# A Mamba-and-attention block: products in halves of rows, and where transposes and turned scores stand

## What is computed

```python
xn = layernorm(x)
# branch 1: D_INNER 512
u = xn @ W_in + b_in
u = causal_conv(u, conv_w, 4 taps) + conv_b
h = tanh(A) h + u_t * Bp;  y_t = Cp h + Dp u_t     # 16 states, scanned over 512 steps
branch1 = silu(y) @ W_out + b_out
# branch 2: 16 heads of 16 columns
q, k, v = xn @ W_qkv + b_qkv
attn = softmax(q k^T / 4) @ v
gate = softmax(xn @ W_gate + b_gate);  combine = the two largest of 8, others 0
branch2 = attn + sum_e combine[e] * (xn @ W_experts[e] + b_experts[e])
out = x + branch1 + branch2
```

## Time and profile before

| | |
|---|---|
| median of 3 runs | 786.23 us (785.99 to 787.51) |
| span of the profiled execution | 784.0 us |
| the profiled execution's own time | not listed beside its span |
| PE busy | 756.4 us, 96% |
| VectorE busy | 582.2 us, 74% |
| ScalarE busy | 534.5 us, 68% |
| GpSimd busy | 389.7 us, 50% |

### The profile page before, as it was taken

One profiled execution on the slowest core, in us unless ns is written; L12 is line 12 of the kernel. 1 busy time (PEld: TensorE's weight loads), 2 busy tenths in 40 slices (PEclk: granted clock), 3 DMA queues, 4 the chain that ended last, 5 costly groups with the idle time before them and its releaser, 6 DMA issues.

```text
span 784.0 us, 13236 instructions
## 1 busy us (share of the span) xinstructions
PE 756.4 (96%) x4408; PEld 455.7 (58%) x4408; DVE 582.2 (74%) x846; ACT 534.5 (68%) x926; POOL 389.7 (50%) x522
## 2 busy tenths in 40 slices
PE   9889999999999999999999999989999999999996
PEld 7566656566555665556555565556655565555553
DVE  6679785977679765897759877698767987568920
ACT  5546775676666766777667776667666776767775
POOL 8347482456344834455346373445444473435654
PEclk9979999999999999999999999999999999999999
DMA  8302111122110221102111121103111111112000
GB/s 272 68 8 66 46 24 30 30 69 69 35 29 22 69 69 41 42 15 82 42 42 42 42 86 32 39 23 96 42 42 43 42 49 41 46 39 69 22 2 27
DMA packets 32465, 39.09 MB, mean 50 GB/s; under 512 B 8513, under 2 KB 18535, under 8 KB 32398
## 3 DMA queue, kind: packets, MB, share of 16 engines
q1 hardware_dynamic: 31418, 37.29, 18.1%
q10 hardware_dynamic: 980, 0.96, 0.6%
HBM read 8.74 MB, written 4.19 MB: 17 GB/s over the span
## 4 chain that ended last, share of the span: by engine, by line
PE 80%; DVE 13%; issue 3%; POOL 2%; ACT 2%; DMA 0%; ACTq 0%; DVEq 0%; POOLq 0%
PE PS L464 38%; PE PS L624 13%; PE SB L591 12%; PE TB L608 7%; PE PS L521 4%; DVE mx L1049 4%; DVE xn L1026 2%; DVE ys L900 2%; PE PS L480 2%; DVE qkl L926 1%; POOL acc L1118 1%; PE PS L631 1%; DVE xl L932 1%; PE PS L476 1%; PE PS L555 1%
## 5 line engine op out<-in xcount | busy, mean ns | idle before, releaser
L1049 DVE TENSOR_REDUCE mx<-SB 128x2 f32<-128x1024 f32 x256 | 312.6, 1221 | 145.2 <-PE SB L591 144.3
L1118 POOL TENSOR_TENSOR acc<-acc,mt 128x256 f32<-128x256 f32 x320 | 252.7, 798 | 244.4 <-ACT mt L674 181.7
L827 ACT ACTIVATE Pt<-TB 128x1024 f32<-128x1024 f32 x251 | 257.5, 1026 | 58.1 <-PE TB L608 54.5
L674 ACT ACTIVATE mt<-PS,cpad 128x256 f32<-128x256 f32 x256 | 107.4, 470 | 58.5 <-PE PS L464 56.5
L591 PE MATMUL SB<-kst,qst 48*128 48x512 f32 x512 | 128.2, 497 | 12.1 <-DVE mx L1049 11.7
L624 PE MATMUL PS<-Pt,V 128*17 128x512 f32 x1024 | 122.3, 595 | 0.0
L591 PEld LDWEIGHTS SB<-kst,qst 48*128 48x128 f32 x512 | 47.8, 183 | 122.4 <-DVE mx L1049 70.3
L464 PE MATMUL PS<-weh,xTh 128*128 128x512 f32 x256 | 109.8, 429 | 1.9 <-DVE xTl L913 1.2
L608 PE MATMUL TB<-qst,kst 50*128 50x512 f32 x502 | 101.3, 399 | 1.3 <-ACT Pt L827 1.3
L464 PE MATMUL PS<-wel,xTh 128*128 128x512 f32 x256 | 100.9, 394 | 0.0
L464 PE MATMUL PS<-weh,xTl 128*128 128x512 f32 x256 | 100.7, 393 | 0.0
(11 more groups left out here) (162 smaller groups left out, 1138.9 us busy)
## 6 DMA issues: line engine op xcount, KB each, us to landing
qst<-qkh SPq DMA_DIRECT2D x124, 64.0 KB, 2.3
kst<-qkh SPq DMA_DIRECT2D x124, 64.0 KB, 2.3
out<-acc SPq DMA_DIRECT2D x8, 512.0 KB, 2.8
qst<-qkl SPq DMA_DIRECT2D x62, 64.0 KB, 2.2
kst<-qkl SPq DMA_DIRECT2D x62, 64.0 KB, 2.3
acc<-in_x SPq DMA_DIRECT2D x7, 512.0 KB, 3.9
Bt<-in_wexp SPq DMA_DIRECT2D x2, 512.0 KB, 8.0
raw<-in_wexp SPq DMA_DIRECT2D x2, 512.0 KB, 8.5
```

Source lines behind the costliest of these rows:

```text
L674: return e.activation(mt[:, item % NM, :], P, ACT.Copy, scale=scale)
L827: e.activation(Pt[:, T % NP, :, :], turned_bank(T)[:, :, :], ACT.Exp, scale=0.25).then_inc(s_ex, 1)
L1049: e.tensor_reduce(mx[:, g % 2, 0:2, 4 * jj + a], SB[:, :, :], AX.X, ALU.max).then_inc(s_mx, 1)
L1118: e.tensor_tensor(v, v, mt[:, item % NM, :], ALU.add).then_inc(s_mt, 1)
```

## The change

Products of V, Q, Z, Y, M and O are issued as halves of 64 rows. `side_by_side(u)` issues the lower halves (rows 0:64) of unit u, and between them the upper halves (rows 64:128) of the unit ahead, whose lower ones are done (s_low); low and high count the columns that each half of the array has been given, and an upper half is issued when its count is behind. Upper ones that are left stand between the two products of the next pair of scores. The planner knows for each unit where it starts and where it is done (ENDS), and a unit keeps its bank for both. X and P move to t divisible by 8 behind the values, T and C to t % 8 == 4 behind values; LAG is 12, so values also stand at t divisible by 4. In a step with two split units `turned` stands between them, otherwise behind `score` as before. X is a plain product of 16 columns in place of a transpose of 72. Z's results have tiles of their own (before they lay over xh and xl). The planner's costs are changed, and the scratch size for DMA descriptors is 1024 rather than 8192.

```diff
-LAG = 11
+LAG = 12
...
+SETTLE = 1500
-COST = {"T": 0.45, "V": 0.75, "Q": 1.42, "Z": 2.05, "Y": 1.42, "C": 0.45, "M": 1.42, "O": 1.5, "B": 0.25, "D": 1.42,
-        "X": 0.15, "P": 0.45}
-
-VECTOR = {"T": {1: 0.7}, "V": {1: 0.2}, "Q": {1: 0.8}, "Z": {1: 1.4}, "P": {1: 0.7}, "X": {1: 0.3},
-          "Y": {2: 1.1, 3: 1.1, 4: 1.1, 5: 1.1, 6: 0.85}}
+Unit = namedtuple("Unit", "kind b i t done read bank use frees item before split")
+
+COST = {"T": 0.45, "V": 0.72, "Q": 1.38, "Z": 1.95, "Y": 1.38, "C": 0.45, "M": 1.38, "O": 1.5, "B": 0.25, "D": 1.42,
+        "X": 0.2, "P": 0.45}
+
+VECTOR = {"T": {1: 0.7}, "V": {2: 0.2}, "Q": {2: 0.8}, "Z": {2: 1.4}, "P": {1: 0.7}, "X": {1: 0.3},
+          "Y": {3: 1.1, 4: 1.1, 5: 1.1, 6: 1.1, 7: 0.85}}
...
+def normal_at(t):
+
+    g, rest = divmod(t - LAG - 12, 8)
+    if t == STEPS + LAG + 2:
+        return NG - 1
+    return g if rest == 0 and 0 <= g < NG - 1 else None
+
+
+def in_halves(kind, b, i, t):
+
+    return kind in "VQZYMO" and t > 1 and (kind, b, i) != LAST
...
-        return 0.43 * pairs + 0.8 * len(values_at(t))
+        return 0.23 * pairs + 1.1 * len(values_at(t))
+
+    def whole_at(t):
+
+        return t % 8 == 4 or t < LAG
...
-        spent = min(spent, 1.0) + share + 0.7 * max(vector[t] - share, 0.0) - fixed(t) - sum(COST[u[0]] for u in row)
+        spent = min(spent, 1.0) + share + 0.35 * max(vector[t] - share, 0.0) - fixed(t) - sum(COST[u[0]] for u in row)
...
+        g = normal_at(t)
+        if g is not None:
             row.append(("P", g // 4, g))
+        halves = 0
+        while t != STEPS + LAG - 2:
+            k = next((k for k, u in enumerate(todo) if soonest(*u) <= t
+                      and (whole_at(t) if u[0] in "TC" else not values_at(t))), None)
+            if k is None:
+                break
+            if todo[k][0] not in "TCB" and (spent < COST[todo[k][0]] / 2 - 1.2 * bare or len(row) > 2):
...
+            if in_halves(*u, t):
+                if open_ is not None:
+                    done[open_] = t
+                open_ = u
+                halves += 1
+            else:
+                done[u] = t
...
+        if open_ is not None and not halves and not values_at(t):
+            done[open_] = t
+            alone.add(t)
+            open_ = None
...
+            bank = min((j for j in range(3) if j != open_), key=lambda j: used[j])
+            used[bank] = place[key]
...
-    return AT[t - 1][-1:] if t - 1 in AT else []
+    return ENDS[t - 1][-1:] if t - 1 in ENDS else []
...
+        zh = sb("zh", [128, 2, 512], F32R)
+        zl = sb("zl", [128, 2, 512], F32R)
...
-        mx = sb("mx", [128, 2, 9, 8])
+        mx = sb("mx", [128, 2, 2, 8])
...
+            def products(u):
+
+                P, b, i = FB[u.bank], u.b, u.i
+                xh_, xl_ = xTh[b % 2], xTl[b % 2]
+                if u.kind == "V":
+                    ts = slice(128 * i, 128 * i + 128)
+                    for f in range(2):
+                        for v, w in ((xh_, wvh), (xl_, wvh), (xh_, wvl)):
+                            yield P[:, 0:264], v[:, f, ts], w[:, f, :], True
...
+            def rest_of_ahead(until=None):
+
+                nonlocal ahead, done, high
+                while ahead and (until is None or high <= until):
+                    o, a, w, _ = ahead_rows[done]
+                    if done == 0:
+                        e.wait_ge(s_low, lower_done)
+                    ins = e.matmul(o, a[64:128], w[64:128], start=False, stop=(done == len(ahead_rows) - 1),
+                                   skip_group_check=True)
+                    high += max(w.shape[1], 256)
+                    done += 1
+                    if done == len(ahead_rows):
+                        ins.then_inc(s_full[ahead.bank], 1)
+                        ahead = None
+
+            def side_by_side(u):
+
+                nonlocal ahead, ahead_rows, half, done, low, high, settled, slots, lower_done
+                rest_of_ahead()
+                ahead, done, high, lower_done = half, 0, max(high, settled), slots
+                half = u
+                if ahead is None:
+                    high = low
+                else:
+                    ahead_rows = [p for p in products(ahead) if p[3]]
+                if u is None:
+                    return rest_of_ahead()
+                start = True
+                for o, a, w, _ in products(u):
+                    rest_of_ahead(low - 1)
+                    ins = e.matmul(o, a[0:64], w[0:64], start=start, stop=False, skip_group_check=True)
+                    start, settled = False, low + SETTLE
+                    low += max(w.shape[1], 256)
+                ins.then_inc(s_low, 1)
+                slots += 1
+                rest_of_ahead(low - 1)
+
+            def bank_there(u):
+                if u.before is not None:
+                    if ahead is not None and ahead.bank == u.bank:
+                        rest_of_ahead()
+                    e.wait_ge(*bank_read(u.before))
...
+                    ins = e.matmul(P[0:16, 0:128], mx[:, i % 2, :, :].rearrange("p h c -> p (h c)"), ident[:, :],
+                                   start=True, stop=True)
...
             def score(t):
...
                 for h in range(2):
                     rows = slice(64 * h, 64 * h + 48)
+                    if h:
+                        rest_of_ahead()
...
                 ins.then_inc(s_S, 1)
+                pair_behind()
...
+            def pair_behind():
+                nonlocal low, high
+                low, high = max(low + 512, high), max(low, high) + 512
 
             def values(m):
+                nonlocal low, high
                 g, a = m // 4, m % 4
+                rest_of_ahead()
+                low = high = max(low, high) + 2200
...
+                between = [u for u in AT[t] if u.split][1:]
+                if LAG <= t < STEPS + LAG and not between:
                     turned(t - LAG)
                 for m in values_at(t):
                     values(m)
+                if t in ALONE:
+                    side_by_side(None)
                 for u in AT[t]:
-                    unit(u)
+                    if between and u is between[0] and LAG <= t < STEPS + LAG:
+                        turned(t - LAG)
+                    if u.split:
+                        bank_there(u)
+                        operands_there(u)
+                        side_by_side(u)
+                    else:
+                        unit(u)
...
-                e.wait_ge(*full("Z", b, 0))
+                    if b and i == 0:
+                        e.wait_ge(*full("Y", b - 1, 3))
+                    e.copy(zh[:, i, :], P[:, :]).then_inc(s_zh, 1)
...
-                    e.wait_ge(*full("Y", b - 1, 3))
+                    e.wait_ge(*full("Z", b - 1, 1))
...
+                    e.wait_ge(s_zh, 2 * b + i + 1)
+                    ins = e.tensor_tensor(zl[:, i, :], P[:, :], F(zh[:, i, :]), ALU.subtract)
```

More of the change, by code:

```diff
@@ L44 @@
          1: [("Q", 0), ("Q", 1)]}
+LAST = ("M", NB - 1, 15)
 def values_at(t):
@@ L152, in plan @@
+    finish = {u: (t, t + (k == len(row) - 1)) for t, row in ends.items() for k, u in enumerate(row)}
+    place = {u: n for n, u in enumerate(u for row in ends.values() for u in row)}
+    units, item, uses, frees, held = {}, 0, [0] * 3, [0] * 3, [None] * 3
+    used, open_ = [-9] * 3, None
     for t, row in steps.items():
         units[t] = []
-        for k, (kind, b, i) in enumerate(row):
-            bank = min((j for j in range(3) if free[j] <= t), key=lambda j: used[j])
-            n += 1
-            used[bank] = n
+        if t in alone:
+            open_ = None
+        for key in row:
+            kind, b, i = key
+            split = in_halves(*key, t)
+            bank = min((j for j in range(3) if j != open_), key=lambda j: used[j])
+            used[bank] = place[key]
@@ L158, in plan @@
             uses[bank] += 1
             frees[bank] += kind not in "MO"
[L160 to L165 removed]
+            u = Unit(kind, b, i, t, *finish[key], bank, uses[bank], frees[bank], item, held[bank], split)
@@ L166, in plan @@
             item += 2 * (kind in "MO")
             held[bank] = u
+            if split:
+                open_ = bank
             units[t].append(u)
-    return units, xh, ln
-AT, XH, LN = plan()
+    return units, {t: [next(u for u in sum(units.values(), []) if (u.kind, u.b, u.i) == k) for k in row]
+                   for t, row in ends.items()}, alone, xh, ln
+AT, ENDS, ALONE, XH, LN = plan()
 UNIT = {(u.kind, u.b, u.i): u for units in AT.values() for u in units}
@@ new lines, in in_one @@
+            def in_one(u):
+                rows = list(products(u))
+                for k, (o, v, w, _) in enumerate(rows):
+                    ins = e.matmul(o, v, w, start=(k == 0), stop=(k == len(rows) - 1))
+                return ins
+            def rest_of_ahead(until=None):
[11 more added lines that the diff above has]
+                        ahead = None
@@ L637, in _ @@
```

(3 more changed lines are left out.)

210 lines of the change are left out of this document (98 added, 112 removed).

## The result

The changed kernel takes 810.65 us (median of 4 runs, 807.96 to 812.04); the kernel before, measured beside it, 786.87 us (785.99 to 788.19). The ratio is 1.0299, with a 95% interval from 1.0276 to 1.0323: slower by 24 us, where 746 was forecast and 714 to 778 was the range.

A forecast was written before the change was run, and what follows sets the result against it. PE was taken as the bound, by its own work. Halves save 77 us, less 3 and 12, so 62; waits return 22: 784.0 - 62 + 22 = 744 as span, 746 as median; range 714 to 778.

The forecast's parts named there:

- a one-unit step: PE's step of scores, turned scores and one unit was to go from 2.25 to 1.85 us.
- Rivals 3 and 4: PE pays each half product's fixed part (38 us back, 784, chance 0.04); or exposes 0.05 per slot in loads (840, 0.09).
- The term for the transposes: X, P, T and C behind values on PE: added shape changes and exposed loads cost 12 us, ends 0 and 19.
- the gain of the halves: On PE, 192 steps each lose 0.40 us of drains and exposed loads: 77 us saved.
- term (b): Split units hold banks over two unit times, so readers get one instead of two: 12 us, bounds 0 and 45.
- rival 5: On PE, upper halves are left over and run alone; costed like the badly hidden loads and counted in their 0.09.
- (a) Maximum: Next scores wait for VectorE's maximum, delayed by convolution taps in shortened steps: 7 us of waits.
- (c) SyncE's queue: Stack DMAs and the block's store come late in SP's queue: 10 us, bounds 0 and 30.
- the first steps: Steps before about 20 wait for weight loads and DVE and give no gain: 3 us off the saving.
- overlap: Waits on maximum, banks and SP's queue let other engines catch up: of 29 us, 22 counted.
- rivals, 2: Queue of banks and stacks takes most, at two thirds of its bounds, 50 us: 774, chance 0.16.
- The one slower case: On PE, the two halves hide each other's loads badly, 0.05 us per slot, 94 us: 840, chance 0.09.

The follow-up runs named there:

- e10: Changed kernel with VectorE reading banks before the convolution taps, turned scores always straight behind the scores, and halves only from step 17 on: 789.63 us.
- e12: e10 with P, T and C in the places they had in the kernel before: 821.32 us.
- e1: Changed kernel with no unit split (whole products); LAG 12, places and new planner costs stay: 810.91 us.
- e2: e1 with units taking only two banks in turn instead of three: 843.71 us.
- e17: e1 with VectorE reading the bank before the convolution tap: 808.45 us.
- e4: Changed kernel with VectorE reading the bank of the unit that ended last before the step's convolution taps: 791.33 us.
- e7: Changed kernel with the three shifted convolution taps over only 8 columns: 787.51 us.
- e8: Kernel before with the three shifted convolution taps over only 8 columns: 778.05 us.
- e13: Kernel before with LAG 12 instead of 11, and the plan that it leads to: 807.21 us.
- e5: e1 with the planner's old costs, VectorE load table, fixed part and weight: 800.30 us.
- e11: e10 with the planner's old weight of VectorE's load, 0.7 for 0.35: 812.67 us.
- e9: e5 with P, T and C where they stood before, X staying behind values: 805.69 us.
- e14: Changed kernel with LAG 11; values, P and X moved to t % 8 == 7, T and C to t % 8 == 3: 820.21 us.

## Why the prediction was wrong

**What was right.** The halves' work on PE: pairs 0.23 apart, no drains, a one-unit step 1.86 for 1.85. X and P behind values at 2.63 for 2.61. Rivals 3 and 4 don't occur: the 1878 further products cost PE neither their fixed part nor exposed loads where both halves run. The rule of the Trainium skill, TensorEngine Tiling (Array Packing), Instruction Overhead, that each matmul carries about 60 cycles, isn't borne out for pairs by these starts either. The term for the transposes is 47 x 0.20 + 32 x 0.10 = 12.6, written as 12; nothing hangs on it.

**Two steps failed.** They are the gain of the halves, put at 77 us and measured at 33, and term (b), the banks, put at 12 us and measured at 33.

**The gain of 77 was too large.** It took a split unit to run in pairs always. Counted as for e10 to e12, between 100 and 770 us of the changed kernel, one half of the array runs alone for about 54 us and neither for 95. In e1 these are 4 and 115, drains and waits together. So halves take some 21 us of standing away, and since a half that runs alone does half the work of its slot, about 25 of the 50 more are lost: that is why e1 and the changed kernel come out the same. That was rival 5's condition ("uppers are left over and run alone"), which I counted with rival 4 at a price per instruction, and so had no term for in the sum. Measured at about equal time to read, halves gain 33 us (e2 against the changed kernel), not 77; their net gain is nothing in the order of the changed kernel and 17 us with reading first (e17 against e4), where the forecast's 77 less 12 for the banks would be 65.

**(b) Banks, 12 taken, 0 to 45 as bounds.** The sentence that failed is "I take 12, since ACT and DVE catch up in the values steps". One unit time less to read costs 33 us (e1 to e2), and the matmuls of the changed kernel wait 42 us for bank readers, against 4 before. The catching up fails at least in part because X and P are now in those values steps and need banks there themselves: P behind qkl alone makes PE wait 9.9 us in 10 of them. The mechanism and the upper bound were right, the value lay in the wrong part of the range. The order of VectorE's queue should have had its own place in the estimate: a reader behind a tap and a maximum is some 2 us late (both durations are in the earlier trace rows), in a step of 1.86.

**(a) Maximum, 7.** The matmuls' own waits on the maximum didn't grow: 9.0 us in 13, against 11.7 in 16. VectorE's lateness came out as bank waits instead. Small taps take 23 us off the changed kernel (e7) and 9 off the one before (e8): the taps cost 14 more than they did.

**(c) SyncE's queue, 10.** Right in kind, too large at the scores. They wait for the stack once:

```profile
PE SB L702 <- DMA kst<-qkl: 0.9, 1, 0.9
```

LAG = 12 in the kernel before costs 20 us with its new plan (e13). Its trace shows late copies of queries that wait for the stacks, X behind values, and units in other steps; I had priced a delay of one step at what it does to one queue. In the changed kernel the copies of queries wait 0.2 us, so there that part is not the price. Who reads what in the step that a phase moves to was the missing term.

**Planner's costs, 0.** 10.6 us for whole products (e5 against e1). The prediction gave them no term and no reason; but they decide which steps hold two units, and e11 shows 23 us for one weight.

**The clock, not foreseen.** I took 1.00 from the earlier trace rows for the whole kernel. See below.

**How it adds up.** Before 787; LAG 12, costs and places make it 811 (e1); one unit time less to read makes it 844 (e2); halves take it back to 811. The measured time is 65 us over the forecast: 44 are the halves' gain (77 less 33), 21 are (b) (33 less 12). The rest nearly cancels, and by luck: the forecast had 25 us for the first steps, the transposes, the maximum and SyncE's queue (3 + 12 + 7 + 10, less 7 for overlap), and e1 shows 24, but by LAG, costs and plan, which had no term. The forecast's direction needed the halves' gain to be larger than the two losses. Of the rivals, 2 had the nearest mechanism, with 774 by its price. The one slower case had the wrong mechanism: it charged PE's own work, while the banks were charged at most 45. With (b) at what it measured and e13's 20 us, the forecast's own sum would have been 746 + 21 + 20 = 787, no gain. What stays open is how the 24 of e1 divide within the plan; e9, e11, e12 and e14 show that single edits come with plans that cost as much.

## What to carry to other kernels

Here one engine was 96% busy and two others near 70%, and shortening its steps didn't move the end. When steps get shorter, look at the readers' order: who reads a buffer should stand ahead of work that nobody waits for (19 us here, for no work), though this only brought the kernel back to the time of before. A scheme that makes a unit hold its buffer over two unit times cost about as much here as one buffer taken away (33 us), so try that first, with whole products, by one number. And when an edit comes with a new delay and new planner costs, take each alone: here they lost 24 us by themselves. Where a planner lays out the kernel, compare the plans too, or hold the plan fixed: an edit of one number moved 245 of 368 units.

## What was unexpected of the hardware

**Matmuls of two row groups.** Lower and upper halves with different weights and different banks start 0.03 apart (422.27 and 422.30) and each pair keeps 0.23, like one whole product. 1878 more matmuls add nothing where pairs are complete.

**TensorE's clock falls in the steady part too.** By stretch: us, busy time (with counts) of PE, PEld, DVE, ACT, POOL, then the granted clock. First the changed kernel, 40 to 100 us and the stretch behind P's wait of 2.06 at 453, which begins 0.3 us ahead of the fall:

```profile
40.00:100.00 60.00, 50.04 (x324) 37.12 (x325) 37.45 (x63) 24.89 (x46) 22.02 (x27) 0.82 0.10 26
...
453.40:456.80 3.40, 3.40 (x18) 2.66 (x18) 2.23 (x4) 1.02 (x1) 0.13 (x1) 0.55 0.02 5
```

The kernel before, 40 to 100 us:

```profile
40.00:100.00 60.00, 56.50 (x285) 37.02 (x285) 49.67 (x82) 37.31 (x69) 32.67 (x37) 0.94 0.16 39
```

In the changed kernel the clock falls to its lower level, 1.2 GHz, at 255.8, 286.5 and 453.7 us for 3.4 us each, and several times between 37 and 81 us. In the kernel before it does so at 37.0 and 47.2 and at the end only. Ahead of two of the changed kernel's three falls behind 100 us a wait of PE stands: 2.06 for P before 453.7, and 1.60 for a bank before 286.5:

```profile
284.98 0.38 PE L622 MATMUL PS<-be,cT 64*128 64x256 f32 x1 [1.60 <-DVE G L1056]
```

Ahead of 255.8 I found no single long one. In the chain of work behind the fall at 453.7 the products of a unit cost 0.42, and 0.22 once the level is back (start, duration, engine, tile, line):

```profile
454.93 0.42 PE PS L622
455.35 0.42 PE PS L622
...
458.56 0.22 PE PS L622
```

By these numbers a fall of 3.4 us costs up to 1.7 (an estimate: half of its length). Three times that is 5 us in the steady part. The first 100 us come on top: over the whole profiled run the granted clock is 0.978 against 0.992 before, that is 18 and 6 us lost by the same estimate. So up to 12 of the 24 us may pass through the clock; in e1 (0.987), which is as slow, it is up to 4. No run holds the clock fixed, so what it really costs is not shown.
